# Shifted-window block with a convolution behind it: second MLP layer in the other orientation, new orders and PSUM banks, and value weighing with the heads innermost

## What is computed

```python
xs = roll(layer_norm(x), (-3, -3)); wins = windows(xs)          # 49 tokens a window
q, k, v = split(wins @ qkv_w + qkv_b)                           # 3 heads of 32
attn = softmax(q * scale @ k.T + bias + mask)
out = roll(unwindow((attn @ v) @ proj_w + proj_b), (3, 3))
x = x + out
y = gelu(layer_norm(x) @ fc1_w + fc1_b) @ fc2_w + fc2_b         # 96 -> 384 -> 96
z = relu(x + y)
z = depthwise3x3(z) + dw_bias
z = z @ pw_kernel + pw_bias
z = z * inv + (beta - moving_mean * inv)
```

## Time and profile before

| | us |
|---|---|
| median of 3 runs | 6512.59 (6494.89 to 6518.01) |
| profiled execution, device time | 6505.5 |
| its span in the profile | 6503.7 |
| PE busy | 5885.1 |
| DVE busy | 5637.3 |
| ACT busy | 5164.0 |
| POOL busy | 3072.3 |

### The profile page before, as it was taken

The page is one execution under the profiler, slowest core; times in us unless marked ns, Lnnn a source line. Parts: engine busy times, 40 slices in busy tenths (PEclk is TensorE's granted clock), DMA queues, the critical chain, the costliest instruction groups (busy, mean ns, idle before and its releaser), DMA issues.

```text
span 6503.7 us, 219980 instructions
## 1 busy us (share of the span) xinstructions
PE 5885.1 (90%) x88850; PEld 4606.4 (71%) x88850; DVE 5637.3 (87%) x14257; ACT 5164.0 (79%) x11040; POOL 3072.3 (47%) x4105
## 2 busy tenths in 40 slices
PE   6999999999999999999999999999999999999997
PEld 4777777777777777777777777777777777777775
DVE  4888888888888888888888888888888888888887
ACT  4888788888878888888888887878888888888785
POOL 3444444444444444444444444444444444445452
PEclk8999999999999999999999999999999999999998
DMA  0111111111111111111111111111111111110100
GB/s 21 26 26 26 26 26 26 26 26 26 26 26 26 26 26 26 26 26 26 26 26 26 26 26 26 26 26 26 26 26 26 26 26 26 26 27 25 28 25 19
DMA packets 250594, 169.04 MB, mean 26 GB/s; under 512 B 220423, under 2 KB 220920, under 8 KB 249592
## 3 DMA queue, kind: packets, MB, share of 16 engines
q1 hardware_dynamic: 249592, 154.97, 9.3%
HBM read 77.81 MB, written 77.07 MB: 24 GB/s over the span
## 4 chain that ended last, share of the span: by engine, by line
PE 66%; DVE 14%; POOL 12%; ACT 4%; issue 3%; SPq 1%; DVEq 0%; DMA 0%; POOLq 0%; ACTq 0%
PE bank L376 17%; PE bank L392 15%; PE bank L422 8%; POOL rstd L881 6%; DVE stats L773 5%; PE bank L452 5%; PE bank L407 5%; POOL x1n L887 5%; PE bank L478 4%; DVE x L819 4%; PE bank L359 4%; PE bank L464 3%; PE bank L344 3%; PE bank L440 3%; ACT attnT L596 2%
## 5 line engine op out<-in xcount | busy, mean ns | idle before, releaser
L757 DVE SCALAR_TENSOR_TENSOR acc<-ymap,taps,acc 96x784 f32<-96x784 f32 (+2 forms) x2176 | 2428.3, 1121 | 45.7
L881 POOL TENSOR_TENSOR rstd<-var_eps,minus_half 112x7 f32<-112x7 f32 x512 | 919.5, 1796 | 3267.0 <-DVE var_eps L788 3267.0
L376 PE MATMUL bank<-x1T,w 96*128 96x448 f32 (+1 forms) x3072 | 1178.0, 523 | 1.5 <-ACT x1T L561 1.2
L392 PE MATMUL bank<-w,hT 128*112 128x96 f32 x10752 | 1099.1, 262 | 0.0
L392 PEld LDWEIGHTS bank<-w,hT 128*112 128x112 f32 x10752 | 1077.9, 178 | 0.6
L376 PEld LDWEIGHTS bank<-x1T,w 96*128 96x128 f32 x3072 | 559.9, 195 | 516.9 <-issue 336.8
L573 ACT ACTIVATE hT<-bank,bfc 128x448 f32<-128x448 f32 (+1 forms) x1536 | 829.3, 576 | 47.6 <-PE bank L376 35.3
L866 POOL TENSOR_TENSOR prob<-prob,smax 128x392 f32<-128x392 f32 x768 | 804.6, 1079 | 21.9 <-DVE smax L726 21.9
L551 ACT ACTIVATE x1n<-x,offset,rstd 112x96 f32<-112x96 f32 x1024 | 394.8, 456 | 388.8 <-POOL offset L884 388.8
L819 DVE TENSOR_TENSOR x<-bank,x_in 112x384 f32<-112x384 f32 (+1 forms) x512 | 250.1, 507 | 468.4 <-PE bank L478 468.4
L875 POOL TENSOR_TENSOR prob<-prob,srec 128x392 f32<-128x392 f32 x768 | 633.2, 855 | 38.6 <-DVE srec L735 38.6
(11 more groups left out here) (89 smaller groups left out, 10996.5 us busy)
## 6 DMA issues: line engine op xcount, KB each, us to landing
out<-o_tile SPq DMA_DIRECT2D x256, 210.0 KB, 2.5
x_in<-in_x SPq DMA_DIRECT2D x256, 168.0 KB, 2.9
x_in<-in_x SPq DMA_DIRECT2D x256, 126.0 KB, 3.3
out<-o_tile SPq DMA_DIRECT2D x256, 84.0 KB, 2.5
hT<-in_L_conv_rel_bias SPq DMA_DIRECT2D x49, 0.6 KB
x1T<-in_L_conv_fc_w SPq DMA_DIRECT2D x1, 144.0 KB, 2.4
w<-in_L_conv_fc_w SPq DMA_DIRECT2D x1, 144.0 KB, 2.3
hT<-in_L_conv_qkv_w SPq DMA_DIRECT2D x1, 108.0 KB, 2.1
```

The source lines that it names most:

```text
L376: pe.matmul(bank[5 + i % 3][:, 0:n * PT_], w1[:, m * 128:(m + 1) * 128], x1T[:, first * PT_:(first + n) * PT_], start=True, stop=True).the ...
L392: mm = pe.matmul(bank[half][0:PT_, a * C:(a + 1) * C], hT[:, m, j * PT_:(j + 1) * PT_], w2[:, m, :], start=(m == 0), stop=(m == MC - 1))
L757: last = dve.scalar_tensor_tensor(out=dst, in0=src, scalar=taps[:, i:i + 1], in1=dst, op0=ALU.mult, op1=ALU.add)
L881: pool.tensor_tensor(b["rstd"][:], b["var_eps"][:], minus_half[0:PT_], ALU.pow)\
```

## The change

- `second_layer` is turned round: `w2` is stationary and `hT` moves, six products of 448 or 336 columns, so the output has channels on the partitions. `x1` is added in the same bank: seven transposes of `x1` are written first, and the products accumulate on them. `add_x1` and `turn_y` are gone, and `into_map` reads the bank of `second_layer`.
- `weigh_values` waits for all three `probT` and runs with the heads innermost.
- Both halves of `values` run ahead of `turn_x1`; `turn_x` runs in one piece after `weigh_values`; `pointwise` and `outputs` are split, the first half ahead of `hidden` and the gelus, the second ahead of `project` and behind `attention_out`.
- On ScalarE both `keys` stand ahead of `normalise(1)`, and `into_map` stands around the copies of the turned probabilities.
- On GpSimd `root` is cut in two: the three tiles of `xn` (`rest`) now come after `divide`. On VectorE tap 4 comes after `add_up`.
- `ymap` has six areas in place of five, and `into_map` waits for the taps of one strip earlier. Banks are dealt anew.

```diff
-            def second_layer(t):
+            def second_layer(t, half):
...
-                    for a in range(n):
-                        j = first + a
-                        for m in range(MC):
-                            mm = pe.matmul(bank[half][0:PT_, a * C:(a + 1) * C], hT[:, m, j * PT_:(j + 1) * PT_],
-                                           w2[:, m, :], start=(m == 0), stop=(m == MC - 1))
-                    mm.then_inc(y_psum, 1)
+                for a in range(n):
+                    pe.matmul(bank[b][0:C, a * PT_:(a + 1) * PT_], x1[:, first + a, :], ident[0:PT_, 0:PT_],
+                              is_transpose=True, start=(a == 0), stop=False)
+                for m in range(MC):
+                    wait(pe, h_ready, nth(t - 1, 6, 3 * half + m))
+                    mm = pe.matmul(bank[b][0:C, 0:n * PT_], w2[:, m, :], hT[:, m, first * PT_:(first + n) * PT_],
+                                   start=False, stop=(m == MC - 1))
+                mm.then_inc(y_psum, 1)
...
-            def weigh_values(t, phase, h):
...
+            def weigh_values(t, phase):
+                wait(pe, v_ready, nth(t, 2, 1))
+                wait(pe, h_ready, nth(t - 1, 6, 4))
+                wait(pe, pt_ready, nth(t, 3, 2))
                 for q in range(QUADS):
                     for side in range(2):
...
+                        at = (2 * q + side) * NT
+                        for h in range(HEADS):
+                            for odd in range(2):
...
             def step(t, phase):
                 if has(t - 1):
+                    root(1, t - 1)
                     wait(pool, x1t_psum, nth(t - 2, 2, 1))
-                    root(1, t - 1, x1n, x1, x1n_rest)
-                shift(t, 0)
-                shift(t, 1)
-                shift(t, 2)
+                    rest(1, x1n, x1, x1n_rest)
+                for g in range(3):
+                    shift(t, g)
+                if has(t + 2):
+                    root(0, t + 2)
+                for g in range(3):
+                    divide(t, g)
                 if has(t + 2):
                     wait(pool, xt_psum, nth(t + 1, 2, 1))
-                    root(0, t + 2, xn, x_in[:, (phase + 2) % UNROLL], xn_rest)
-                for g in range(3):
-                    divide(t, g)
+                    rest(0, xn, x_in[:, (phase + 2) % UNROLL], xn_rest)
```

More of the change, by code:

```diff
@@ L54 @@
 AREA = 10
-AREAS = 5
+AREAS = 6
 TOP_ROWS, LOW_ROWS = 5, 2
@@ L410, in turn_probs, with turn_x @@
                 mm.then_inc(pt_psum, 1)
-            def weigh_values(t, phase, h):
[L413 to L416, removed]
+            def weigh_values(t, phase):
+                wait(pe, v_ready, nth(t, 2, 1))
+                wait(pe, h_ready, nth(t - 1, 6, 4))
+                wait(pe, pt_ready, nth(t, 3, 2))
                 for q in range(QUADS):
                     for side in range(2):
[L419 to L428, removed]
+                        at = (2 * q + side) * NT
+                        for h in range(HEADS):
+                            for odd in range(2):
+                                rows = slice(64 * odd, 64 * odd + NT)
+                                mm = pe.matmul(bank[5 + odd][h * HD:(h + 1) * HD, at:at + NT],
+                                               vw[rows, phase % 2, q, side, h * HD:(h + 1) * HD],
+                                               probT[rows, h, q, 64 * side:64 * side + NT], start=True, stop=True)
+                mm.then_inc(o_psum, 1)
+            def turn_x(t):
                 if not has(t + 2):
@@ L444, in pointwise @@
+            def pointwise(t, phase, i):
                 if not has(t - 4):
                     return
[L446 to L449, removed]
+                first, n = HALVES[i]
+                if not has(t):
                     wait(pe, out_ready, nth(t - 5, 2, i))
[L451 to L466, removed]
+                if i == 0:
+                    wait(pe, tap_done, nth(t - 4, 9, 8))
+                    wait(pe, q_ready, nth(t + 1, 2, 1))
+                else:
+                    wait(pe, s_biased, nth(t, 3, 2))
@@ L468, in project @@
+                for a in range(n):
+                    mm = pe.matmul(bank[(4, 2)[i]][0:HW, a * C:(a + 1) * C], acc[:, phase % 2, first + a, :], wpw[:],
+                                   start=True, stop=True)
+                mm.then_inc(pw_psum, 1)
             def project(t):
@@ L486, in step @@
                 values(t, 0)
+                values(t, 1)
                 turn_x1(t)
-                values(t, 1)
+                pointwise(t, phase, 0)
                 hidden(t, 0)
                 hidden(t, 1)
-                pointwise(t, phase)
-                second_layer(t)
-                turn_x(t, 0)
+                second_layer(t, 0)
+                second_layer(t, 1)
                 if has(t):
@@ L496, in step @@
                         turn_probs(t, h)
-                turn_x(t, 1)
-                if has(t):
-                    for h in range(HEADS):
-                        weigh_values(t, phase, h)
-                turn_y(t)
+                    weigh_values(t, phase)
+                turn_x(t)
+                pointwise(t, phase, 1)
                 project(t)
@@ L614, in into_map @@
                 s = t - 1
-                wait(act, tap_done, nth(t - 3, 9, 8))
+                first, n = ((0, 4), (4, 3))[half]
+                if half == 0:
+                    wait(act, tap_done, nth(t - 4, 9, 8))
                 area = area_of_strip(s)
@@ L837, in step @@
                 tap(t, phase, 3)
-                tap(t, phase, 4)
                 for g in range(3):
                     add_up(t, g)
-                add_x1(t)
-                for i in range(5, 9):
+                for i in range(4, 9):
                     tap(t, phase, i)
@@ L885, in root, with rest @@
                     .then_inc(scale_ready[which], 1)
+            def rest(which, dst, src, done):
+                b = ln[which]
                 for j in range(ACT_NORM, WS):
```

161 lines of the change are left out of this document (76 added, 85 removed).

## The result

| | before | changed |
|---|---|---|
| median of 4 runs, us | 6508.42 | 8420.07 |
| ratio, 95% interval | | 1.294 (1.2925 to 1.2956) |
| span of the profiled execution | 6503.7 | 8425.2 |
| mean granted clock of TensorE | 0.987 | 0.702 |

The account below looks back on a forecast made before the run. No engine alone bounds it: two thirds of the waits lie on PE, the rest loops over VectorE, GpSimd and ScalarE. From 6505.5, -32 clock, about -3 tail, 0 for steps: 6470, compared as 6475; range 6245 to 6640 us.

Parts of the forecast that it names:

- the term for TensorE's clock: Ahead of `turn_x1`: idle gap shrinks from 1.18 to 0.4 us, so 22 clock falls of 1.47 us go, -32 us.
- rival (b): Around weighing and ahead of `turn_x`: 2.65 us idle within 4.3 drops TensorE's clock, 1.47 us a time; chance 0.25.
- the turn-taking of taps and GpSimd: VectorE taps and GpSimd divides and `xn` tiles block each other; tiles end at 3021.1, one per 1.07 us tap.
- The wait ahead of `turn_x1`: On TensorE, the second half of `values` (0.80 us) fills this 1.18 us wait, leaving about 0.4.
- The central sum: Whole kernel: step change about 0, -32 us clock, about -3 tail, giving 6470, or 6475 to compare; chance 0.38.
- Rival (a): GpSimd's third divide or `xn` tiles not held up by taps: 150 to 230 us less, 6245 to 6325; chance 0.27.
- Rival (c): Weighing stays at 21 ns a record: +0.25 us a step, 6540 us; chance 0.10 including unseen waits like it.

Follow-up runs that it names:

- g2_perhead: Changed kernel with the weighing put back head by head, each head waiting only for its own copy of the turned probabilities: 6516.05 us, 1.0022.
- e2_fill: Changed kernel plus 5, 3 and 4 unread products in TensorE's waits ahead of the third turned probability, the weighing and `turn_x`: 6519.45 us, 1.0024.
- e1_rest_early: Changed kernel with GpSimd's three tiles of `xn` put back ahead of the three divides: 6584.68 us, 1.0135.
- e3_heads_outer: Changed kernel with only the weighing's loop order put back, head by head, still waiting for all three copies: 7336.58 us, 1.1269.
- f4_fill_transposes: Changed kernel with 8, 5 and 7 unread transposes ahead of the third turned probability, the weighing and `turn_x`: 6512.22 us, 1.0023.

## Why the prediction was wrong

**The step that failed is the term for TensorE's clock: the price and the chance of rival (b).** The sum had the clock at -32 us, and (b) said: the price is 1.47 a time, 6850 if every step catches it. Rival (b) had the mechanism and its place right: three waits within 4.3 us (0.89, 0.77 and 0.73 us for the 1.1, 0.65 and 0.9 expected), and the fall there, in every step. The price was read from the falls of before, which came at the start of `hidden` and mostly ended after 3.4 us. Here the stretch begins ahead of `project` and lasts 13.7 to 23.9 us. The steps of the changed kernel with 13.7 us of it take 30.3 us, those with 17.1 take 31.7 and those with 23.9 take 34.3, against 25.0 with the clock held: 5.3 to 9.3 us a fall, not 1.47. By means over all steps, from the first and last copy to `attnT` of the changed kernel and of g2_perhead,

```profile
L588 ACT COPY attnT<-bank x256: 221/236/259, 77.8 to 8371.3; 96x21 f32<-96x21 f32 x128
```

```profile
L588 ACT COPY attnT<-bank x256: 224/242/267, 78.2 to 6463.8; 96x21 f32<-96x21 f32 x128
```

the step is 32.52 and 25.04: 7.5 us a step, which in 256 steps is all of the 1912.

**The evidence against (b) was misread.** I took the 3.4 us with 2.09 busy around the first weighing as a sign that weighing alone holds the clock. That weighing lasted 2.01 us and had one wait behind it, not three around it. The changed one lasts 1.1 to 1.25, and I counted its 0.8 us as saved without asking what it did to the share of busy time in a place that I had just called thin. The chance of 0.25 and the range, which stopped at four steps in ten, follow from both.

**What held.** On the clock of before, with the end of `turn_x1` at 3005.94, and in the changed kernel with 3017.67:

| behind the end of `turn_x1`, us | expected | measured |
|---|---|---|
| first divide starts | 8.81 | 8.79 |
| third divide ends | 11.96 | 11.99 |
| tiles of `xn` end | 15.16 | 15.34 |
| weighing starts | 13.1 | 13.46 |

The tiles took 3.37 us in place of 1.24 and the turn-taking of taps and GpSimd was as the earlier trace rows had it. The weighing was 1.1 us with the clock up. The wait ahead of `turn_x1` went down to 0.46 (e2_fill). `second_layer` with its transposes was 4.6 us and not the 5.2 that I took: in the chain of e2_fill its six products took 3.96 and its transposes 0.68; since TensorE was waiting anyway, that gained nothing.

**The central sum** said 0 a step and 6475 with the clock held. The runs with the clock held by fills or by the old weighing have 6512 to 6519 and a step of 25.0, 0.27 more than before: `xn` was 0.2 later than the sum had it. So that part was off by 40 us, less than 1%.

**Rival (a)**, GpSimd not held up, did not happen in the changed kernel: the third divide took 1.59 us and the tiles 3.37. With the late tiles taken away by another order, in e1_rest_early, the plain step was 24.3 against 25.0, the 0.7 that (a) had been priced at. **Rival (c)**, the weighing no quicker, did not happen either.

**Open.** What sets the length of a low stretch. In the changed kernel those of 13.7 us end at the end of the keys and those of 23.9 in `hidden`, that is in or behind products of 392 and 448 columns without a wait; before, `hidden` stood right behind the fall. No run here parted the width of the products from the absence of waits. And what follows does not decide it alone: 48 of the 72 low stretches of e1_rest_early and 129 of the 201 of e3_heads_outer last 3.4 us, though most of these begin in the weighing too, ahead of the same `pointwise` and `project`. Nor is it settled why the two waits ahead of the weighing were worth more than the one behind it; with the late `xn` in place, no run filled only one of the two.

## What to carry to other kernels

On a queue that feeds TensorE, a short wait can have two prices: its own length, and that of all that follows at half clock if the work around it gets thin. Before an edit that gathers waits in one place, or makes TensorE's work between two waits shorter, compare how densely TensorE works there with the thinnest place of the kernel before. Do not price a fall by the falls seen elsewhere in the kernel: here one cost 0.6 us in e1_rest_early, 1.5 in the kernel before and up to 9.3 in the changed kernel. What stands behind it, taken at half speed, is the safer bound. If the clock has fallen, products that nobody reads, put into the waits, tell within one run whether the clock is the loss; then move the late work (here three tiles on GpSimd from behind the divides to ahead of them) so that the wait goes.

## What the runs showed of the hardware

- No single wait of TensorE ahead of the falls of the changed kernel was over 0.9 us, and the clock fell in every step. With the same 96 weighing records at 2.01 us in place of 1.25 and the wait of 0.77 ahead of them gone, it stayed at 2.4 GHz between waits of 0.89 and 0.81 us (g2_perhead).
- A low stretch that began at the weighing lasted anything from 3.4 us (e1_rest_early, a step of 24.9 for 24.3) to 23.9 (the changed kernel, 34.3 for 25.0).
- With the waits filled by transposes alone the clock stayed at 1.00 between 100 and 6400 us (f4_fill_transposes). The Trainium skill (TensorE: Matmul & The Clock Gate, Part 4: PE-mode transpose) says that they do not count as busy in the same way and that full clock does not engage for them; here, put between other products, they held it, in mean at 0.994 against 0.702 without them.
- The speed of small tiles by their order: 96 records of the weighing took 2.01 us head by head and 1.08 with the heads innermost (e2_fill), 21 and 11 ns a record.
- A tap with two inputs in SBUF and a GpSimd instruction held each other up in both directions: tiles of 0.41 us took 1.12 beside taps and a divide of 0.85 took 1.59, and five taps, 5.35 us at the 1.07 of the earlier trace rows, took 6.21.
